# Convolution as three fp32r products, state-space tables eight heads at a time, first layer's tokens by head, x1 written by batch to its own memory

## The reference

```python
def _L0_cond_ref(u, log_dt, C, log_A_real, A_imag, D, length):   # u: 64, 32, 512
    dt = jnp.exp(log_dt)
    A = -jnp.exp(log_A_real) + 1j * A_imag
    dtA = A * dt[:, None]
    Ct = Cc * (jnp.exp(dtA) - 1.0) / A
    K = 2.0 * jnp.einsum('hn,hnl->hl', Ct, jnp.exp(dtA[:, :, None] * jnp.arange(512))).real
    y = causal_convolution(u, K) + u * D[:, None]      # the reference does it by FFT
    return y * mask[:, None, :]                        # position < length of the batch
def _L0_ffn_ref(x, ...):   # block scales; 512 -> 1792 -> 512
    return (silu(x @ w1.T) * (x @ w3.T)) @ w2.T
x = x + _L0_ffn_ref(_L0_cond_ref(x, ...), ...)         # x1
x = x + _L1_ffn_ref(_L1_cond_ref(x, ...), W, b)        # 512 -> 1376 -> 512 with rank 16 per batch, then ternary
```

## Time and profile before

| what | value |
|---|---|
| time, median of 3 runs | 1183.92 us (1183.47 to 1184.62) |
| profiled execution: span | 1183.3 us from first to last instruction |
| profiled execution: own time | not listed apart; the runs lie 0.2 to 1.3 us above the span |
| PE busy | 1100.2 us, 93% of the span |
| DVE, ACT, POOL busy | 541.0, 306.6, 139.0 us |
| first gate product of layer 0 | 69.57 us after the start |
| mean granted TensorE clock | 0.980 |

### The profile page before, as it was taken

How to read it: one execution, slowest core, us unless ns; L and a number is a source line. 1 busy time by engine, 2 the same in 40 slices (tenths; PEclk the granted TensorE clock), 3 DMA queues, 4 the chain that set the end, 5 groups by cost and what they waited for, 6 DMA issues and landing times.

```text
span 1183.3 us, 13353 instructions
## 1 busy us (share of the span) xinstructions
PE 1100.2 (93%) x5306; PEld 900.6 (76%) x5306; DVE 541.0 (46%) x652; ACT 306.6 (26%) x486; POOL 139.0 (12%) x184
## 2 busy tenths in 40 slices
PE   0689999999999999999999999999999999997774
PEld 0467778888888888888888888888888888886651
DVE  6423534444334344444564334343353343456876
ACT  1222222121211212122342122221222221123665
POOL 7300000000000000000031010100101001013425
PEclk9989999999999999999989999999999999998987
DMA  5322301010010101011041012112102111022103
GB/s 203 127 71 71 106 1 54 1 45 9 0 53 0 53 0 53 0 33 56 14 147 55 27 54 80 42 38 80 53 27 93 40 68 65 27 87 91 46 1 142
DMA packets 19213, 65.42 MB, mean 55 GB/s; under 512 B 3922, under 2 KB 4210, under 8 KB 18930
## 3 DMA queue, kind: packets, MB, share of 16 engines
q1 hardware_dynamic: 13554, 39.88, 9.3%
q0 software_dynamic: 5632, 25.17, 6.7%
HBM read 60.76 MB, written 4.28 MB: 55 GB/s over the span
## 4 chain that ended last, share of the span: by engine, by line
PE 88%; DVE 4%; POOL 3%; issue 2%; ACT 2%; DMA 1%; DVEq 0%; POOLq 0%; ACTq 0%
PE ps_gu L141 18%; PE ps_gu L140 18%; PE ps_gu L142 17%; PE ps_d L140 8%; PE ps_d L141 8%; PE ps_d L142 8%; PE ps_t L599 3%; PE ps_gu L599 3%; PE ps_t L140 1%; PE ps_t L142 1%; PE ps_t L141 1%; POOL sm L412 1%; PE ps_gu L822 1%; DVE h_lo L1474 1%; PE ps_t L713 1%
## 5 line engine op out<-in xcount | busy, mean ns | idle before, releaser
L140 PE MATMUL ps_gu<-a_hi,gu_hi 128*128 128x512 f32 x800 | 318.7, 398 | 3.2 <-DVE a_lo L1213 3.2
L141 PE MATMUL ps_gu<-a_lo,gu_hi 128*128 128x512 f32 x800 | 317.8, 397 | 0.0
L142 PE MATMUL ps_gu<-a_hi,gu_lo 128*128 128x512 f32 x800 | 315.9, 395 | 0.0
L140 PEld LDWEIGHTS ps_gu<-a_hi,gu_hi 128*128 128x128 f32 x800 | 152.6, 191 | 36.3 <-DVE a_lo L1213 3.4
L142 PEld LDWEIGHTS ps_gu<-a_hi,gu_lo 128*128 128x128 f32 x800 | 151.3, 189 | 34.8
L141 PEld LDWEIGHTS ps_gu<-a_lo,gu_hi 128*128 128x128 f32 x800 | 151.9, 190 | 30.7
L1328 DVE TENSOR_TENSOR s_act<-s_act,ps_gu 128x512 f32<-128x512 f32 x44 | 30.2, 687 | 193.7 <-PE ps_gu L142 193.4
L1235 DVE TENSOR_TENSOR s_act<-s_act,ps_gu 128x512 f32<-128x512 f32 x56 | 38.5, 687 | 168.2 <-PE ps_gu L142 168.2
L308 POOL DMA_INDIRECT lr_raw<-in_tab_l,rows x48 | 45.9, 956 | 367.7 <-PE ps_t L713 347.2
L140 PE MATMUL ps_d<-h_hi,dn_hi 128*128 128x512 f32 x224 | 87.8, 392 | 0.0
L141 PE MATMUL ps_d<-h_lo,dn_hi 128*128 128x512 f32 x224 | 87.5, 391 | 0.0
(11 more groups left out here) (219 smaller groups left out, 1634.6 us busy)
## 6 DMA issues: line engine op xcount, KB each, us to landing
raw<-in_w SPq DMA_DIRECT2D x26, 768.0 KB, 5.7
toep<-krev SPq DMA_DIRECT2D x3, 2048.0 KB, 7.9
acc<-in_x_t SPq DMA_DIRECT2D x1, 4096.0 KB, 17.9
out<-acc SPq DMA_DIRECT2D x16, 256.0 KB, 2.0
toep<-krev SPq DMA_DIRECT2D x2, 1024.0 KB, 7.3
w_all<-in_wq SPq DMA_DIRECT2D x1, 1024.0 KB, 10.4
raw<-in_wq SPq DMA_DIRECT2D x4, 256.0 KB, 4.3
lr_raw<-in_tab_l,rows POOLq DMA_INDIRECT x48, 4.0
```

Of the source, the lines that this page charges most:

```text
L140: pe.matmul(out_ap, st_hi, mv_hi, start=start, stop=False, skip_group_check=skip)
L141: pe.matmul(out_ap, st_hi, mv_lo, start=False, stop=False, skip_group_check=skip)
L142: return pe.matmul(out_ap, st_lo, mv_hi, start=False, stop=stop, skip_group_check=skip)
```

## The change

Four things are changed together. (1) The convolution takes x and its kernel as high and low halves and makes three fp32r products of each fp32 one; the Toeplitz matrix is read twice, from `krev_hi` and `krev_lo`, in quarters of two heads. x is loaded, and split by ACT and DVE, a tile at a time. (2) The state-space tables are made for eight heads at a time with two buffers: POOL makes angles and magnitudes, DVE the coefficients (until now POOL's) and the tables; the kernels of tiles 2 and 3 are made inside chunk 0. (3) In layer 0 tokens stand by head (h, b), so that a tile is 512 words in a row. (4) x1 is written in the last chunk by batch to a memory of its own, `x1b`, one instruction per tile (two for the last), and split a group of 256 tokens at a time, two groups ahead of the projections.

```diff
-        "x_t": a["x"].reshape(TOK, L).T.reshape(KB, P, TOK).transpose(1, 0, 2),
+        "x_t": a["x"].transpose(2, 1, 0).reshape(KB, P, TOK).transpose(1, 0, 2),
...
+        x1b = sb("x1b", [P, KB, TOK])
+        x1b4 = x1b[:].rearrange("p k (b h) -> p k h b", h=HEADS)
...
+                def toeplitz(t):
+                    sp.wait_ge(s_kw[t], 32)
+                    for q in range(4):
+                        if t:
+                            sp.wait_ge(s_conv, 4 * (t - 1) + q + 1)
+                        for i, dst in enumerate((toep_hi, toep_lo)):
+                            sp.dma_start(dst[:, 2 * q:2 * q + 2].bitcast(F32),
...
+                pool.wait_ge(s_step, 1)
+                angles(0)
...
+                angles(1)
+                pool.wait_ge(s_pw, 1)
+                magnitudes(0)
+                magnitudes(1)
+                for t in range(2, NT):
+                    angles(t)
+                    magnitudes(t)
...
-                                last = pe.matmul(bank[:, i, d:KB, :], toep[:, hh, L - P * (d + 1):L - P * d],
-                                                 acc4[:, 0:KB - d, :, t * HPT + hh], start=(d == 0), stop=True,
-                                                 skip_group_check=True)
+                                last = mm3(pe, bank[:, i, d:KB, :], toep_hi[:, hh, lags], toep_lo[:, hh, lags],
+                                           a_hi4[:, 0:KB - d, h, :], a_lo4[:, 0:KB - d, h, :],
+                                           start=(d == 0), stop=True, skip=True)
...
-                                mv = (a_hi4[:, k, :, t * HPT:(t + 1) * HPT], a_lo4[:, k, :, t * HPT:(t + 1) * HPT])
+                                mv = (a_hi[:, k, t * TT:(t + 1) * TT], a_lo[:, k, t * TT:(t + 1) * TT])
...
+                        if first and t == 0:
+                            for n in range(2, NT):
+                                state_sums(n)
                         if first and t + 1 < NT:
                             conv(t + 1)
...
-                                if first and u == 0 and w == 0:
-                                    pe.wait_ge(s_x1l, KB * (NT - 1) + k + 1)
+                                if w == 0 and k == 0:
+                                    pe.wait_ge(s_x1l, 2 * i + (u + 1))
...
+                sines(0)
+                x_high(0)
+                sines(1)
+                kernel_high(0)
+                sines(2)
+                kernel_high(1)
+                sines(3)
                 for f in range(2):
                     act.wait_ge(s_wsc[f], 1)
...
+                        if not last_pair:
+                            at = bass.ds(i * (2 * GT) + (2 + u) * GT, GT)
+                            act.activation(a_hi[:, :, at], x1b[:, :, at], ACT.Copy).then_inc(s_x1h, 1)
...
+                state_tables(0)
+                state_tables(1)
+                kernel_low(0)
+                x_low(0)
+                kernel_low(1)
...
+                        if last_chunk and t == NT - 1:
+                            for sl, s_done in ((slice(0, GB), s_evk), (slice(GB, BATCH), s_ev)):
+                                dve.tensor_tensor(x1b4[:, :, hs, sl], acc4[:, :, hs, sl], ps_heads[:, :, :, sl],
+                                                  ALU.add).then_inc(s_done, 1)
...
+                        if not last_pair:
+                            ahead = bass.ds(i * (2 * GT) + (2 + u) * GT, GT)
+                            dve.wait_ge(s_x1h, 2 * i + (u + 3))
+                            dve.tensor_tensor(a_lo[:, :, ahead], x1b[:, :, ahead], a_hi[:, :, ahead].bitcast(F32),
+                                              ALU.subtract).then_inc(s_x1l, 1)
```

More of the change, by code:

```diff
@@ L110, in build @@
         raw = sb("raw", [P, 2, 3, L])
+        with ExitStack() as state_space:
+            scope[0] = state_space
+            par_sb = sb("par_sb", [P, 4, HEADS])
+            e3 = sb("e3", [P, 3, HEADS])
+            sm = [sb(f"sm{i}", [P, HEADS]) for i in range(8)]
+            nri = sb("nri", [P, 2, HEADS])
+            wri = sb("wri", [P, 2, HEADS])
+            prod = sb("prod", [P, 2, 2, HEADS])
+            pin = sb("pin", [P, 9, HEADS])
+            pw = sb("pw", [P, 9, HEADS])
+            tmp = [sb(f"tmp{i}", [P, 9 * HEADS]) for i in range(4)]
+            kint = sb("kint", [P, 9 * HEADS], I32)
+            trig_small = (sb("sin1", [P, HEADS])[:], sb("sin2", [P, HEADS])[:])
+        scope[0] = top
         s_act = sb("s_act", [P, 2, TT])
@@ L210, in build @@
[L210 to L219, removed]
@@ L225, in build @@
+            scope[0] = layer0
+            w_all = sb("w_all", [P, KB * L])
+        scope[0] = top
+        x1b = sb("x1b", [P, KB, TOK])
+        z = x1b[:].rearrange("p k t -> p (k t)").rearrange("p (s n) -> p s n", n=L)
         pk = ps_d[0:NA, :, 0:HPT * NB].rearrange("a t (h b) -> a t h b", b=NB)
         a_hi4, a_lo4, acc4 = by_head(a_hi), by_head(a_lo), by_head(acc)
+        x1b4 = x1b[:].rearrange("p k (b h) -> p k h b", h=HEADS)
         conv_bank = (ps_t[:], ps_gu[2])
-        acc_tile = [acc4[:, :, :, t * HPT:(t + 1) * HPT] for t in range(NT)]
@@ new lines, in magnitudes @@
+                def magnitudes(t):
+                    hs = slice(t * HPT, (t + 1) * HPT)
+                    mg = mag[:, t % 2]
+                    if t >= 2:
+                        pool.wait_ge(s_sf, 3 * (t - 1))
+                    pool.memset(mg[:, :, NA - 1:NA], 1.0)
+                    link(pool.memset(mg[:, :, NA + NB - 1:NA + NB], 1.0))
+                    for e, first, doublings in ((NA + NB, 0, 5), (NA, 5, 4)):
+                        for k in range(doublings):
+                            n = 1 << k
+                            tt(mg[:, :, e - 2 * n:e - n], mg[:, :, e - n:e], bc(pw[:, first + k, hs], 2, n), ALU.mult)
+                    pool.sem_inc(s_mag, 1)
@@ L931, in _, with x1_high @@
                 chunk(NC0 - 1, False, True)
+                def x1_high(g):
+                    act.activation(x_group(a_hi, g), x_group(x1b, g), ACT.Copy).then_inc(s_x1h, 1)
+                act.wait_ge(s_evk, 1)
+                x1_high(0)
+                act.wait_ge(s_ev, M1)
+                x1_high(1)
                 def split(u, n):
@@ L1198, in _, with first_weights @@
                     dve.tensor_tensor(w, w, bc(scale0[:, f], 2, P), ALU.mult).then_inc(s_wsc[f], 1)
-                for f in range(2):
+                def first_weights(f):
                     dve.wait_ge(s_whg[f], 1)
@@ L1245, in chunk @@
                                                   ALU.subtract).then_inc(s_wlg[f], 1)
+                        if first and t == 0:
+                            kernel_low(2)
+                            kernel_low(3)
                         if first and t + 1 < NT:
                             masked(t + 1)
+                        if first and t + 2 < NT:
+                            x_low(t + 2)
                         if t == 1 and not last_chunk:
@@ L1280, in chunk @@
                                                   ALU.subtract).then_inc(s_wld[f], 1)
+                masked(0)
+                x_low(1)
+                for n in range(2, NT):
+                    state_tables(n)
+                chunk(0, True, False)
                 dve.wait_ge(s_id, 2)
                 dve.tensor_copy(ident_b[:], ident_f[:]).then_inc(s_id, 1)
-                masked(0)
-                chunk(0, True, False)
                 dve.wait_ge(s_wall, 16)
```

404 lines of the change are left out of this document (215 added, 189 removed).

## The result

The changed kernel takes **1156.5 us** (median of 4 runs, 1153.5 to 1157.0), the kernel before 1184.0 beside it (1183.5 to 1184.6): ratio 0.9761, 95% interval 0.9747 to 0.9775. The profiled execution's span is 1154.5 instead of 1183.3. It is faster, and 0.9 us from the number predicted; but one of the reasons was wrong, and the experiments were spent on that.

A forecast was written before the change was run, and what follows sets the result against it. PE, busy 93% of the span, and the wait chain before the first gate product bound the kernel; -11.1 - 20.3 + 3.9 - 8.9 + 3.8 + 6.1 = -26.5 from 1183.92 gives 1157.4 us, range 1143 to 1174.

The forecast's parts named there:

- The start: Everything before the first gate product, paced by POOL's list: first gate product at 58.5 instead of 69.6 us, -11.1.
- The one-input instruction for which there was no row: POOL instruction in each tile's angles at the start: taken as 0.95 us, between 0.6 and 1.3.
- the exclusion: At the start, POOL and two-SBUF-input DVE instructions exclude each other only while columns pass; rival, whole instructions: 1164.6, chance 0.15.
- the quarters then follow the transfers at 3.2, and the last ends at 54.8: First convolution, tile 0: its quarters are paced by Toeplitz matrix transfers, 3.2 us per MB, the last ending at 54.8.
- The convolution: Tiles 1 to 3: short fp32r products at 0.109 to 0.12 make a tile 10.7 instead of 17.5 us, -20.3 in all.
- the rival without a gain: Convolution: short fp32r products win nothing over fp32, a tile stays at 17.5 us, total 1178; chance 0.10.
- Sums of tiles 2 and 3: Kernels of tiles 2 and 3 move into PE's chunk 0, 1.9 us each: +3.9.
- Tokens by head: Gate/up of layer 0: words in a row give all tiles the best time, 10.92; 7 chunks, -8.9.
- Step: From layer 0 to the projections: DVE's adds and splits delay PE's first group to 607.6 from 603.8, +3.8.
- Projections: DVE's list takes 4.93 us a group over PE's 3.80; six groups carry it, +6.1 (0 to +8).
- that rival is out: PE's clock in the projections: DVE-bound groups idle PE, which drops to half clock; some +20, 1177; chance 0.06.

## Why the prediction was right

- **The start** (-11.1; -7.9). The list on POOL, ACT and DVE came as drawn up, with GpSimd's last angles at 49.9 (48) and the mask ended at 54.0 (52.1). The one-input instruction for which there was no row takes 1.92 instead of 0.95, outside its bounds of 0.6 and 1.3; four of them stand in the list, 3.9 us, of which other estimates gave half back. Where the exclusion shows singly, the one that was shut out waited for the whole instruction: an angle product beside x's low half (2.27) took 3.93 instead of 1.27, a hold-up of 2.7 where the prediction had 1.8. The step that failed is "the quarters then follow the transfers at 3.2, and the last ends at 54.8". They ran at 5.1, since PE was at the lower clock level and the prediction had it at the upper one, and the last one had to wait for the mask of the second; each alone gives about the same end, as the runs with one of them taken away show.
- **The convolution** (-20.3; -19.7). The size was right, by the transposes' 0.109 a product, and the rival without a gain is out as a time. The reason was half wrong: it was put down to three short fp32r products, while 7.9 of 17.5 us a tile come from reading words in a row, which the prediction costed at nothing there though it saw the same matter in gate and up. What that rival says, that short fp32r products win nothing over fp32, is true once the words stand in a row: 10.85 against 9.6.
- **Sums of tiles 2 and 3** (+3.9; +2.2). The row for them came from the start, where PE ran at half pace: 1.92 there, 1.10 in chunk 0.
- **Tokens by head** (-8.9; -10.4). Right in cause; words in a row take 10.88, below the 10.92 that was taken.
- **Step** (+3.8; +2.1). The two adds took 3.66, not 4.32, and PE's first group 4.8, not 5.8. **Projections** (+6.1; +6.1): right, in its cause too. The granted clock was 0.50 from 561.8 to 568.6, which is most of the first group, and 1.00 from there to the last mask, so that rival is out.

The two misses that cost (start 3.2, convolution 0.6) were more than met by those that gave (sums 1.7, gate and up 1.5, step 1.7, the rest of layer 0 0.7, layer 1 and the tail 0.5): the profiled span fell by 28.8, not 26.5. That the median came within 0.9 of 1157.4 is in part luck.

## What to carry to other kernels

When one change alters both the number format and the layout of an operand, price the layout by itself: here three quicker products hid that one slow one, read in a row, was quicker still. Count short products by their own rows: the three gained at 256 columns and lost at 128 and 64. Before taking a granted clock of 1.00 at its word, see whether the trace lists any clock there, and set the pace beside it. Where two chains end at the same time, an experiment that shortens one of them says nothing; take both away before calling either harmless. An elementwise operation moved to GpSimd to unload VectorE is only off its path where VectorE's work beside it has an input in PSUM, and whatever GpSimd does next comes later.

## What was not expected of the hardware

- A product of 192 or 256 columns started every 0.17 or 0.22 us with words 128 bytes apart and about every 0.11 to 0.12 in a row; 128 and 64 columns took 0.09 to 0.11 either way. Runs of 8 words cost 0.04 to 0.70 us in 48 products of 512 columns, by the word at which they begin (8 the least, 16 the most).
- In the changed kernel PE worked on short fp32r products from 38.35 to 59.5, with no gap over 0.3 us, and the granted clock rose only at 66.9, 5 us into the gate products of 512 columns; with the sines alone moved it rose at 64.4. With one fp32 product in their place it rose at 44.4, 6 us after the first one, and with spare products of 512 columns from 16.4 on it rose at 21.9. Yet the same short fp32r products ran through tiles 1 and 2, 10.9 us each, at a listed 1.00. Why they keep the clock and don't raise it stays open.
- The GpSimd instruction of one input and 512 columns (L431, two operations in one instruction) took 1.92 us, the ones of two inputs 1.04 to 1.27 where nothing held them up.
- The last chunk, from the same down product to the end, took 135.7, 132.3, 132.5 and 136.2 us in the changed kernel, two of the runs above and the kernel before, and 138.2 in the run with the sines alone moved. The time in it at a granted clock of 0.50 was 32.9, 22.7, 26.2, 33.2 and 39.4 us, so the scatter goes largely with the clock; what sets the clock off there was not tried. Differences under 3 us were therefore read from the stages, not from the whole time.
